# Early tiles' output scattered among the routing's writes, tiles 7 and 8 fetched in a row, gate weights spread by a product, one row of zeros

## The reference

```python
# x: (64, 64, 1024) float32 = 4096 tokens of 1024 features
y   = einsum('bct,bcd->bdt', x, cond_weights[itok])     # per batch, a 64x64 mix of its 64 rows
log = y @ W_gate + b_gate                               # 8 experts
top = top_k(log, 2)                                     # two experts for each token
out = x + mean over the two of relu(y @ W_e[e] + b_e[e])
```

## Time and profile before

| | us |
|---|---|
| median of three runs | 900.36 (897.53 to 901.7) |
| the profiled execution, its own time | 897.66 |
| its span in the trace | 896.0 |
| mean granted clock of PE | 0.986 of full |

### The profile page before, as it was taken

One profiled execution on the slowest core, in us unless ns is written; L12 is line 12 of the kernel. 1 busy time (PEld: TensorE's weight loads), 2 busy tenths in 40 slices (PEclk: granted clock), 3 DMA queues, 4 the chain that ended last, 5 costly groups with the idle time before them and its releaser, 6 DMA issues.

```text
span 896.0 us, 16403 instructions
## 1 busy us (share of the span) xinstructions
PE 850.3 (95%) x4102; PEld 675.5 (75%) x4103; DVE 408.5 (46%) x537; ACT 255.8 (29%) x309; POOL 513.4 (57%) x560
## 2 busy tenths in 40 slices
PE   6899799996999999999999999999999999999992
PEld 3454478885878888888888888888888888888882
DVE  3788756426733373335533373336433733333320
ACT  4565411105511151123321241115211511222210
POOL 2177777647567666654675557555655565555311
PEclk9999999998999999999999999999999999999997
DMA  9999999678965586545854495546664664444433
GB/s 322 416 414 394 391 330 326 177 205 240 304 162 126 108 251 158 113 100 135 249 113 94 94 281 117 103 100 207 175 117 94 187 119 101 96 98 96 78 48 47
DMA packets 54472, 163.23 MB, mean 182 GB/s; under 512 B 14378, under 2 KB 14986, under 8 KB 54442
## 3 DMA queue, kind: packets, MB, share of 16 engines
q0 software_dynamic: 26720, 77.79, 39.6%
q1 hardware_dynamic: 21306, 67.65, 20.9%
q10 hardware_dynamic: 6416, 17.44, 5.0%
HBM read 106.47 MB, written 70.94 MB: 198 GB/s over the span
## 4 chain that ended last, share of the span: by engine, by line
PE 80%; DMA 6%; DVE 5%; issue 4%; POOL 3%; ACT 1%; ACTq 0%; POOLq 0%; DVEq 0%; SPq 0%
PE psO L573 76%; PE psO L509 3%; POOL rows L416 2%; DMA rows<-in_x 1%; DMA out<-rows,first_to 1%; DMA wgc<-wgc 1%; PE psG L521 1%; DVE turned L814 1%; DMA out<-ys,first_to 1%; DMA out<-rows,idx_s 1%; POOL out L430 0%; DMA raw<-in_L_cond_weights 0%; DVE w_lo L827 0%; DMA rows<-y_rows,idx_g 0%; POOL idx_g L412 0%
## 5 line engine op out<-in xcount | busy, mean ns | idle before, releaser
L573 PE MATMUL psO<-w_hi,a_hi 128*128 (+1 forms) x1104 | 343.3, 392 | 11.7 <-DVE a_lo L962 8.8
L573 PE MATMUL psO<-w_lo,a_hi 128*128 (+1 forms) x1104 | 341.1, 390 | 0.0
L573 PE MATMUL psO<-w_hi,a_lo 128*128 (+1 forms) x1104 | 340.9, 390 | 0.0
L416 POOL DMA_INDIRECT rows<-y_rows,idx_g x248 | 256.0, 1032 | 108.0 <-issue 52.7
L573 PEld LDWEIGHTS psO<-w_hi,a_hi 128*128 128x128 f32 x1104 | 207.4, 189 | 55.9 <-issue 11.0
L573 PEld LDWEIGHTS psO<-w_lo,a_hi 128*128 128x128 f32 x1104 | 208.3, 189 | 43.5
L573 PEld LDWEIGHTS psO<-w_hi,a_lo 128*128 128x128 f32 x1104 | 207.9, 188 | 43.2
L962 DVE TENSOR_TENSOR a_lo<-ys,a_hi 128x1024 fp32r<-128x1024 f32 x62 | 75.9, 1224 | 112.7 <-ACT a_hi L700 112.7
L688 ACT ACTIVATE ys<-ys 128x1024 f32<-128x1024 f32 x33 | 35.0, 1061 | 263.0 <-DVE ys L924 263.0
L688 ACT ACTIVATE rows<-rows 128x1024 f32<-128x1024 f32 x33 | 35.0, 1061 | 252.2 <-DVE rows L924 252.2
L924 DVE TENSOR_TENSOR rows<-psO,bias 128x1024 f32<-128x1024 f32 x33 | 40.3, 1222 | 127.8 <-PE psO L573 112.4
(11 more groups left out here) (126 smaller groups left out, 328.4 us busy)
## 6 DMA issues: line engine op xcount, KB each, us to landing
raw<-in_L_ffn_W_e SPq DMA_DIRECT2D x56, 512.0 KB, 6.3
rows<-in_x SPq DMA_DIRECT2D x32, 512.0 KB, 8.8
y_rows<-ys ACTq DMA_DIRECT2D x32, 512.0 KB, 8.8
out<-in_x SPq DMA_DIRECT2D x14, 1024.0 KB, 6.8
bias<-in_L_ffn_b_e SPq DMA_DIRECT2D x8, 512.0 KB
rows<-y_rows,idx_g POOLq DMA_INDIRECT x248, 2.9
raw<-in_L_ffn_W_e POOLq DMA_DIRECT2D x4, 512.0 KB, 8.9
bias<-in_L_ffn_W_e POOLq DMA_DIRECT2D x4, 512.0 KB, 8.8
```

What stands on the lines that cost most here:

```text
L416: pool.indirect_dma_start(out=rows[:, slot, a * DQ:(a + 1) * DQ], out_offset=None, in_=y_parts, in_offset=bass.IndirectOffsetOnAxis(ap=idx ...
L573: last = nc.tensor.matmul(ps[:, h * BANK:(h + 1) * BANK], a[:, p, k * P:(k + 1) * P], w[:, bass.ds(slot + (k * H + h * BANK), BANK)], star ...
```

## The change

1. **Scatters.** `scatter_early(0)` comes after the fetch of early tile 3, `scatter_early(1)` after that of tile 5, `scatter_early(2)` after that of tile 6, each with a wait for only those copies of x that its rows need. The rows of output numbers are now made in `part(t)`, for each early tile by itself.
2. **Tiles 7 and 8.** The two fetches follow each other, ahead of scatter 3. DVE does `ahead(7)` before it transposes tile 8, and the order of its first steps, and ACT's, is drawn forward to match; the loops begin one tile later.
3. **Gate weights.** PE spreads them by one product with `spread` ahead of tile 0, and DVE copies them out of PSUM ahead of its loop; the three transfers are gone. The condition weights are loaded once, and ACT copies them to the other half.
4. **Zeros.** One row of zeros in `y_dram` stands for all empty slots (number 0); the 128 rows behind the output are filled by a copy of 128 rows of x, on SP after `copy(1)`.
5. **Order in the routing stage.** Splits 6 and 7 of the first expert move from tiles 24 and 28 to 23 and 26; `share` and `read_from` move from tiles 22, 26 and 30 to 23, 27 and 31 and have a PSUM bank of their own; early tile 0 is transposed and split from tile 28 on in place of tile 30.

```diff
@@ PSUM and semaphores
-        total_at, from_at = slice(Q * E, Q * E + E), slice(3 * Q * E, 3 * Q * E + Q)
+        psX = pb("psX", [P, BANK])
+        total_at, from_at = slice(Q * E, Q * E + E), slice(0, Q)
...
-        SPLITS = {5: 0, 7: 1, 10: 2, 13: 3, 16: 4, 19: 5, 24: 6, 28: 7}
+        SPLITS = {5: 0, 7: 1, 10: 2, 13: 3, 16: 4, 19: 5, 23: 6, 26: 7}
...
-        SPREAD = {22: 0, 26: 1, 30: 2}
+        PART = {22: 0, 26: 1, 30: 2}
+        SHARE = {23: 0, 27: 1, 31: 2}
@@ sync
-                for i in range(PAIR):
-                    sp.dma_start(cw[C * i:C * (i + 1), :, :], cond_w.rearrange("n c d -> c n d")).then_inc(s_cw, 16)
+                sp.dma_start(cw[0:C, :, :], cond_w.rearrange("n c d -> c n d")).then_inc(s_cw, 16)
...
                 copy(1)
+                sp.dma_start(out[TOK:TOK + P, :], x_rows[0:P, :]).then_inc(s_pad, 16)
                 sp.wait_ge(s_split, KD)
@@ gpsimd
-                pool.dma_start(y_dram[0:P, :], zero).then_inc(s_spare, 16)
-                pool.dma_start(out[TOK:TOK + P, :], zero).then_inc(s_spare, 16)
+                pool.dma_start(y_dram[0:1, :], zero).then_inc(s_spare, 16)
...
                 def scatter_early(t):
+                    for j in range(2):
+                        pool.wait_ge(s_copy[j], (t + 1) * 16)
                     if t:
                         pool.wait_ge(s_add, t * 16)
...
                 early(3)
+                pool.wait_ge(s_pad, 16)
+                scatter_early(0)
                 route(6)
                 early(4)
                 early(5)
+                scatter_early(1)
                 route(7)
                 early(6)
-                for j in range(2):
-                    pool.wait_ge(s_copy[j], (len(left) + 1 - j) // 2 * 16)
+                scatter_early(2)
                 for s in range(G):
                     pool.wait_ge(s_xout[s], 16 * (len(STORES) // G))
-                scatter_early(0)
                 pool.wait_ge(s_idx, 1)
                 gather(tile(0, EARLY))
-                scatter_early(1)
-                scatter_early(2)
                 gather(tile(0, EARLY + 1))
                 scatter_early(3)
@@ tensor
+                pe.wait_ge(s_gw, 16 * Q)
+                pe.wait_ge(s_same, 1)
+                nc.tensor.matmul(psX[:, 0:NB * E], spread[0:R, :], wgc[:, :, :].rearrange("p b e -> p (b e)"),
+                                 start=True, stop=True).then_inc(s_gr, 1)
@@ scalar
-                    if n == 0:
-                        act.wait_ge(s_gw, Q * 16)
-                        for a in range(1, Q):
-                            act.dma_start(wgc[a * R:(a + 1) * R, :, :], wgc[0:R, :, :]).then_inc(s_gr, 16)
...
-                    if n == NTILE - 2:
+                    if n == NTILE - 4:
                         early_hi(0)
...
                 parts(tile(0, EARLY))
+                ahead(EARLY)
                 relu(tile(0, EARLY - 1))
-                ahead(EARLY)
@@ vector, part(t)
+                    to_out(first_to[:, t:t + 1], first_f[:, t:t + 1], behind[:, t:t + 1])
+                    dve.sem_inc(s_to, 1)
@@ vector, the end of the routing loop
+                    if n == NTILE - 3:
+                        early_lo(0)
...
-                    if n == NTILE - 2:
+                    if n == NTILE - 4:
                         turn_early(0)
-                        early_lo(0)
@@ vector, first tiles behind the early ones
                 parts(tile(0, EARLY))
+                dve.wait_ge(s_add, FIRST * 16)
+                ahead(EARLY)
                 turn_rows(tile(0, EARLY + 1))
                 finish_early(EARLY - 1)
-                dve.wait_ge(s_add, FIRST * 16)
-                ahead(EARLY)
+                parts(tile(0, EARLY + 1))
+                returned(tile(0, EARLY + 2))
+                finish_last(tile(0, EARLY))
+                ahead(EARLY + 1)
```

More of the change, by code:

```diff
@@ L112, in build @@
         part_q = sb("part_q", [P, 1])
+        empty_to = sb("empty_to", [P, 1])
         tile_e = sb("tile_e", [1, NL], I32)
@@ L134, in build @@
         ones = raw[:, 2, G * P + P + P // 2:G * P + 2 * P].bitcast(BF16)
-        spare = bias[:, 0:COLS].bitcast(U32)
-        zero = bias[:, H:2 * H]
+        spare = bias[:, 0:COLS]
+        zero = bias[0:1, H:2 * H]
         chunk = [raw[:, 0, :], raw[:, 1, :], bias[:, 0:H], bias[:, H:2 * H]]
@@ L416, in gather @@
                         pool.indirect_dma_start(
-                            out=rows[:, slot, a * DQ:(a + 1) * DQ], out_offset=None, in_=y_parts,
+                            out=rows[:, slot, a * DQ:(a + 1) * DQ], out_offset=None, in_=y_parts[0:(1 + TOK) * Q, :],
                             in_offset=bass.IndirectOffsetOnAxis(ap=idx_g[:, slot, a:a + 1], axis=0)
@@ L610, in _ @@
                     if n in UNSTACK:
-                        unstack(UNSTACK[n], sum(m < n for m in SPREAD))
+                        unstack(UNSTACK[n])
                     if n in RANKS:
@@ L702, in _ @@
                 conditions(0)
+                act.wait_ge(s_cw, 16)
+                nc.scalar.copy(cw[C:P, :, :], cw[0:C, :, :]).then_inc(s_cw2, 1)
+                act.wait_ge(s_cw2, 1)
+                act.wait_ge(s_bd0, 2)
                 for s in range(G):
@@ L789, in _ @@
                 V.tensor_copy(it_f, it_i)
+                own(V.tensor_scalar(empty_to[:, :], short_i[:, :], float(TOK + 1), None, ALU.add))
                 own(V.tensor_scalar(short_i[:, :], short_i[:, :], 5, None, ALU.logical_shift_right))
@@ L962, in parts @@
                     V.tensor_tensor(a_lo[:, p, :], ys[:, p, :], a_hi[:, p, :], ALU.subtract).then_inc(s_alo, 1)
-                def first_out(lo, hi):
-                    to_out(first_to[:, lo:hi], first_f[:, lo:hi], behind[:, lo:hi])
-                    dve.sem_inc(s_to, 1)
+                gate_blocks()
                 for n in range(NTILE):
-                    if n in SPREAD:
-                        part(SPREAD[n])
+                    if n == NTILE - 3:
+                        early_lo(0)
+                    if n in PART:
+                        part(PART[n])
                     if n in UNSTACK:
@@ L1073, in _ @@
                     for c in range(4):
-                        step(i, c, there)
+                        step(i, c + 1, there)
                 split_to(2 * (E - 1))
```

74 lines of the change are left out of this document (34 added, 40 removed).

## The result

The changed kernel takes 894.56 us (median of 10 runs, 892.84 to 897.0), the kernel before 899.13 us (median of 10 runs beside them). The ratio is 0.9948, 95% interval 0.9931 to 0.9965: 4.6 us faster, where the forecast was some 10 us. The profiled execution took 893.59 us with a span of 891.5 us; 888.9 was forecast for it.

A forecast was written before the change was run, and what follows sets the result against it. PE, 95% busy, bounds the kernel, with POOL's stream deciding the early tiles: tile 6 at 185.3 plus 65.2 puts tile 12 at 250.5, not 259.34, 8.8 us less; 888.9 profiled, 889.5 forecast, range 882 to 896.5.

The forecast's parts named there:

- the front's gain: Routing stage: first early tile starts at 101.1 instead of 109.95, expected to be hidden by POOL's stream.
- some 11 us: Early tile 2: PE, there at 130.4, waits this long in one or two pieces for share(5) at 141.4.
- Rival A: Routing stage's gain survives: tile 6 starts toward 172, time 876 at best, 882 with half; chance 0.11.
- the middle: Tiles 7 to 12: new scatter and fetch order and earlier split remove all 11.5 us lost there.
- T6: Start of tile 6, forecast at 185.3 us, before at 182.7; tile 12 follows 65.2 us later.
- rival B: Tiles 8 to 12: late weight chunks cause two or three waits of 1 to 2 us, 895 us; chance 0.14.
- Rival C: Tile 8 waits behind ahead(7) for expert 1's last chunk; landing at 210 gives 903 to 905; chance 0.05.
- Rival D: Experts' last tiles: empty slots all fetch one zero row, reads queue up, 1 us lost each, 897; chance 0.03.
- POOL is 1.5 us later: From fetch 1 on, POOL's stream runs 1.5 us later than before, span -1 to +3.
- 3.3 us of saved traffic: Routing stage: 1.4 MB fewer transfers at 415 GB/s bring its dates 3.3 us forward.
- the landing of SP's read: Read of group 5's slots takes 9.1 us to land, at 140.6, just ahead of share(5).
- the clock's term: PE's clock falls after its wait at share(5), as at tile 8, adding 2.35 us before tile 6.

The follow-up runs named there:

- e13: Changed kernel with scatters, fetches of tiles 7 and 8 and DVE's and ACT's first steps as before, new routing stage kept: 903.42 us, 1.0063 of before.
- e5: The changed kernel itself, measured again: 894.91 us, 0.9944 of the kernel before.
- e6: Kernel before with only scatter placing, tile 7 and 8 fetch order and DVE's and ACT's first steps changed: 892.78 us, 0.9911 of before.
- e15: e8 with one copy of x in flight, and 1, 2 and the rest around slot reads of groups 5 and 6: 909.53 us, 1.0122 of before.
- e7: Changed kernel with shares back at tiles 22, 26, 30 and splits 6 and 7 back at tiles 24, 28: 891.36 us, 0.9907 of before.
- e8: e7 with POOL's load of weight chunk 7 behind route(1) instead of ahead of it: 890.97 us, 0.9901 of before.
- e14: e8 again, unchanged, as base for later runs: 891.85 us, 0.9927 of the kernel before.
- e16: e8 with scatter 0 behind the fetches of early tiles 4 and 5, and scatter 1 behind route(7): 890.79 us, 0.9921 of before.
- e17: Changed kernel with only the shares back at tiles 22, 26 and 30: 892.44 us, 0.9908 of the kernel before.
- e18: e16 with only the third share one tile later (22, 26, 31): 893.86 us, 0.9941 of the kernel before.
- e4: Changed kernel with 2, 4 and the rest of the x copies around slot reads of groups 5 and 6, not 5, 4, 3; slower chip: 938.36 us, 1.0023.
- e10: Same kernel as e15, on the slower chip: 936.21 us, 1.0019 of the kernel before there.
- e11: Same kernel as e16, on the slower chip: 921.54 us, 0.9859 of the kernel before there.
- e1: Same kernel as e13, on the slower chip: 942.5 us, 1.0089 of the kernel before there.

## Why the prediction was right and wrong

**Right: what bounds, and where the front's gain goes.** The prediction said that POOL's stream, not PE, decides when the early tiles' middle can run, that PE would wait there "some 11 us", and that the front's gains would be hidden. PE waited 8.2 us at just that place, and the front alone is slower than before (e13). PE came 6.5 us later than forecast (136.89, forecast 130.4) and `share(5)` 3.8 us later, hence a wait of 8.2 us in place of 11. Rival A, the gain surviving, is out.

**Right: the middle.** T6 + 65.2 us was forecast for tile 12. Measured were 66.1 us from tile 6 to tile 12, and 76.6 before: 10.5 us gone of the 11.5 expected. The one row left is the 1.0 us wait for `a_lo` at tile 12, with no fall of the clock. It has the look of rival B, but not its cause: B had late weight chunks, and the chain above comes from a scatter, whose landing at 250.02 the bias add was waiting for. The scatters, each issued when the one before had landed, took 8.1, 8.1 and 6.0 us to land, so POOL had not caught up before tile 12, which the prediction had taken for granted. Rival C did not occur: DVE's passes on the weights at tile 8 waited 0.84 us. Rival D is out: PE has no wait at any expert's last tile behind 256 us, and from tile 12 to the end of the span it is 636.3 and 637.4 us with one row of zeros (changed kernel, e5) and 636.6 and 637.1 with 128 (before, e6).

**Wrong: the term "POOL is 1.5 us later".** It was 4.6 us at fetch 1 and 4.0 us at group 5's slot write. Two things are in it. First a slip of my own: I worked out when the row numbers would be made (95.5) and compared it with when fetch 1 had been *issued* (93.89); from row numbers to issue are 1.04 us, before (92.85 to 93.89) and after (97.46 to 98.50), so my own terms gave 2.6 and not 1.5. Second, I took 3.3 us of saved traffic and 1.3 us of the first share's wait off the date of `from_q(1)`; it came at 97.46, 2.0 us later than so reckoned. The traffic that went did not speed up the stage. Between 20 and 64 us it moves 416 GB/s with a DMA share of 1.03, as before. Most of what was saved, 0.9 of the 1.4 MB, lay in the first 20 us (6.24 MB before, 5.35 now), and there it left the engines partly idle; before, then changed:

```profile
0.00:20.00 20.00, 14.07 (x60) 7.67 (x61) 8.67 (x22) 8.95 (x21) 6.14 (x21) 1.00 0.89 312
0.00:20.00 20.00, 13.95 (x62) 7.85 (x63) 11.73 (x28) 11.42 (x25) 6.14 (x21) 1.00 0.81 267
```

SP's fifth load of `x` waits for PE's first product, and so it was issued at 10.51 us, before at 10.38; at 61 us, where SP reads the first slots, nothing had been gained (61.27, before 61.25). The forecast had multiplied bytes by a rate and left out that wait. What PE no longer waited for in gate weights (4.4) it waited for in tiles of `x`, 7.7 us where the kernel before has:

```profile
PE psO L509 <- DMA rows<-in_x: 2.7, 7, 0.8
```

Nor did the clock stay up in front: 0.96 from 64 to 110 us, before 1.00. The first early tile began at 106.32, before at 109.95: 3.6 us earlier, and not the 8.8 of the forecast.

**Wrong by less: the landing of SP's read.** 9.1 us was put for it, the median in the earlier trace rows; it took 10.56 in the chain above, inside the 7.2 to 12.0 of those rows. The Trainium skill (DMA: Bandwidth & Descriptors, Anatomy of one DMA — SWDGE path) gives a fixed cost of about 2 us for a DMA of the GpSimd path, most of it the completion. It gives it for that path, and this read is issued by SP, beside copies at 309 GB/s and a DMA share of 1.03. On the usual chips one read alone, the 1.6 us of e15, was that short; on the long chip many were, with medians of 1.6 to 3.7 us. For this chip the trace's rows were the right source.

**The sum by rows.** `share(5)`: forecast 141.4; plus 2.5 (slot write at 128.20 and not 125.7, and the copy in front of SP's read just as late), plus 1.5 (landing) less 0.2 of small differences gives the measured 145.22. T6: 185.3 plus the same 3.8 is the measured 189.1, so the clock's term, 2.35 us, held. Tile 12: 250.5 plus 3.8 plus 0.9 is 255.19. The whole error of 4.7 us is thus 2.5 + 1.5 - 0.2 + 0.9, and on the median it is 894.56 - 889.5 = 5.1 us. The range (882 to 896.5) held the time; of the some 10 us of gain 4.6 came. The step that failed is the term "POOL is 1.5 us later", with 4.6 and 4.0 us in its place, outside its own span of -1 to +3, and after it the landing; the prediction had called these two its weakest numbers.

**What stays open.** In e6, whose front is the one of before but for two small DVE instructions behind each part, fetch 1 came at 98.12, though at 93.89 in the profile of before: this date moved by 4 us with next to nothing changed in the front, and on one profile each it can't be said how often it does. The changed front gave 98.50, 98.37 and 98.28 in three profiles (changed, e5, e13), with the first two shares put back 93.92, 93.17, 94.22, 93.77, 95.02 and 93.54 in six (e7, e8, e14, e16, e17, e18); the medians of e5 and e7 rest on no single date. Why landings and dates scatter so is not known from these runs.

## What to carry to other kernels

Ahead of a wait that is removed or a step that is moved later, follow the queue that stands behind it, instruction by instruction: here shares moved one tile later to spare PE a wait cost 3 to 4 us, because a fetch in POOL's queue hung on their result and all the issues up to the table, at 172.90, stood behind that fetch; one share alone did the same in the profile of e18. Ahead of turning saved bytes into saved time, look whether the next transfer was waiting for the engines or for a step of the kernel. Compare like with like when a date is carried over (made with made, issued with issued). Of two parts of a change, measure each alone; the better kernel here has the middle's part and the shares where they were (891 to 892 us, e7, e8, e14).

## What the runs showed of the hardware that I had not expected

- On one chip the kernel before took some 36 us longer and the others 27 to 43, at the same granted clock in the matmul stream behind 300 us. There PE has waits that name no releaser, in e4 19.5 us in 26 pieces at the gate's matmuls, where the usual chips show none:

```profile
PE psG L525 <- issue: 19.5, 26, 1.5
PE psO L573 <- issue: 6.8, 15, 1.4
```

  Behind 200 us they come to 4.2 us in 6 pieces, and from 300 to 800 us PE is busy throughout at a granted clock of 1.00, as on the usual chip: the loss is in the routing stage. The clock is part of it: 0.80 from 64 to 150 us in e4, 0.92 in the changed kernel on the usual chip. What such a wait is the profile doesn't show. Differences are not carried over between the chips: e10 was 0.2% slower than before there and 1.2% here, e11 1.4% faster there and 0.8% here.
- A read of 0.5 KB took 10.56 us to land beside copies that move 309 GB/s; six of the seven in that kernel, those whose landing the trace shows, lay between 3.1 and 10.6 us. On the long chip such reads were quicker, 1.5 to 1.9 us in e1.
- Taking 1.4 MB off a stage that moves 416 GB/s did not bring its 3.3 us: 0.9 MB of it lay in the first 20 us, where the rate just fell from 312 to 267 GB/s, and the waits moved from one transfer (4.4 us for gate weights) to another (5.0 us more for tiles of `x`).
